# Second half's inputs among the states of the first scan, first half's routing among those of the second, and GpSimd's products of two batches exchanged

## The reference

```python
xz = rmsnorm(x) @ in_proj_w ; xi, z = split(xz)       # 256 channels each
xi = silu(causal_conv4(xi) + conv_b)
dbc = xi @ x_proj_w                                   # 64 dt, 16 B, 16 C
delta = softplus(dt @ dt_proj_w + dt_proj_b)
h[n] = exp(delta * A[n]) * h[n] + delta * xi * B[n]   # 16 states n, over 512 tokens
y = sum_n C[n] * h[n] + D_skip * xi
r = x + (y * silu(z)) @ out_proj_w
out = r + sum of 2 of 8 experts of rmsnorm(r), by the router's weights
```

## Time and profile before

| | us |
|---|---|
| median of 3 runs | 719.82 |
| lowest, highest | 719.0, 720.14 |
| the profiled execution | 721.8 |
| its span in the profile | 720.0 |
| busy in the span: PE, DVE, ACT, POOL | 568.5, 486.4, 385.1, 330.1 |
| TensorE's mean granted clock | 0.92 of full speed |

### The profile page before, as it was taken

The page is one execution under the profiler, slowest core; times in us unless marked ns, Lnnn a source line. Parts: engine busy times, 40 slices in busy tenths (PEclk is TensorE's granted clock), DMA queues, the critical chain, the costliest instruction groups (busy, mean ns, idle before and its releaser), DMA issues.

```text
span 720.0 us, 11031 instructions
## 1 busy us (share of the span) xinstructions
PE 568.5 (79%) x3428; PEld 360.5 (50%) x3447; DVE 486.4 (68%) x1310; ACT 385.1 (53%) x604; POOL 330.1 (46%) x289
## 2 busy tenths in 40 slices
PE   1948587789356776878999899956789989988787
PEld 1413233344112222477989799933555544545366
DVE  5639999944799799643633565387777787886053
ACT  1586555615755455255675566623355665556741
POOL 5249989900599999322578432433012012112010
PEclk9977998799699899889999999985999999999999
DMA  5836565400387765130114200422103103000001
GB/s 141 282 103 196 161 175 164 143 0 7 121 269 232 211 184 180 31 93 15 38 54 126 85 16 22 120 81 80 35 1 93 21 2 101 8 3 2 2 15 45
DMA packets 50523, 65.91 MB, mean 92 GB/s; under 512 B 7730, under 2 KB 29250, under 8 KB 50210
## 3 DMA queue, kind: packets, MB, share of 16 engines
q1 hardware_dynamic: 45122, 59.27, 28.0%
q0 software_dynamic: 2496, 5.15, 1.9%
q10 hardware_dynamic: 2848, 0.78, 0.5%
HBM read 47.46 MB, written 9.52 MB: 79 GB/s over the span
## 4 chain that ended last, share of the span: by engine, by line
PE 33%; POOL 11%; DVE 10%; issue 9%; ACT 4%; ACTq 1%; DMA 0%; POOLq 0%; another core or an unknown queue 0%; DVEq 0%
PE ps L1509 30%; POOL arena L823 4%; DVE arena L1429 3%; POOL moe_out L808 2%; POOL moe_rows L800 2%; ACT arena L1058 2%; POOL arena L835 2%; PE ps L1769 1%; DVE x L1364 1%; DVE nb L1157 1%; DVE arena L1290 1%; DVE stats L1144 1%; POOL arena L849 1%; ACT r L1058 1%; PE ps L1776 1%
## 5 line engine op out<-in xcount | busy, mean ns | idle before, releaser
L1509 PE MATMUL ps<-arena 128*128 128x128 f32 (+10 forms) x2131 | 317.7, 326 | 45.8 <-DVE arena L1429 18.2
L1509 PEld LDWEIGHTS ps<-arena 128*128 128x128 f32 (+2 forms) x2150 | 207.2, 158 | 126.7 <-issue 55.4
L1509 PE MATMUL ps<-arena,ident 128*128 128x512 f32 x256 | 141.6, 703 | 67.0 <-DVE arena L1300 67.0
L1290 DVE TENSOR_TENSOR_SCAN arena<-ps,arena 128x512 f32<-128x512 f32 x128 | 147.9, 1202 | 10.2 <-POOL arena L823 7.2
L1429 DVE CUSTOM_DVE_ANT_0 arena<-ps,cmask 128x128 f32<-128x128 f32 (+3 forms) x256 | 111.3, 487 | 26.4 <-PE ps L1509 25.4
L1509 PEld LDWEIGHTS ps<-arena,ident 128*128 128x128 f32 x256 | 53.9, 222 | 150.2 <-DVE arena L1300 95.3
L999 ACT ACTIVATE ps<-arena 128x512 f32<-128x512 f32 x128 | 87.9, 689 | 73.6 <-DVE arena L1290 73.5
L823 POOL TENSOR_TENSOR arena<-arena 128x1024 f32<-128x1024 f32 x64 | 126.9, 2003 | 0.6
L1058 ACT ACTIVATE arena<-ps 128x1024 f32<-128x1024 f32 (+3 forms) x86 | 57.0, 709 | 37.9 <-PE ps L1509 37.5
L808 POOL DMA_INDIRECT moe_out<-arena,xT x46 | 44.9, 976 | 69.6 <-DVE arena L1453 56.3
L787 POOL TENSOR_TENSOR small<-small,neghalf 128x4 f32<-128x4 f32 (+1 forms) x18 | 22.2, 1236 | 116.3 <-DVE small L1380 75.1
(11 more groups left out here) (191 smaller groups left out, 610.1 us busy)
## 6 DMA issues: line engine op xcount, KB each, us to landing
arena<-bc_rows SPq DMA_DIRECT2D x128, 256.0 KB, 3.9
arena<-arena SPq DMA_DIRECT2D x64, 64.0 KB
arena<-arena SPq DMA_DIRECT2D x28, 128.0 KB, 2.4
moe_rows<-arena SPq DMA_DIRECT2D x2, 1495.0 KB, 11.7
arena<-moe_rows SPq DMA_DIRECT2D x8, 325.0 KB, 5.0
arena<-in_L_attn_a_Wg SPq DMA_DIRECT2D x8, 256.0 KB, 4.9
arena<-in_L_attn_a_Wu SPq DMA_DIRECT2D x8, 256.0 KB, 5.1
arena<-moe_out SPq DMA_DIRECT2D x4, 512.0 KB, 4.3
```

Source lines behind the costliest of these rows:

```text
L1290: V.tensor_tensor_scan(hst[:, g % STATES, e, :], bank(6 + e), dBx[:, g % RING, e, :], 0.0, ALU.mult, ALU.add).then_inc(s_scan, 1)
L1509: return T.matmul(o, l, rr, start=start, stop=stop)
```

## The change

- **Inputs ahead.** The in_proj matmuls and the diagonal-matmul convolution of half 1 are made among the states of half 0, through PSUM bank 5, at the states in AHEAD; ScalarE copies each result at the states in COPY_AT, z into a new buffer `zr` (over weights' staging space that is free by then). Silu of all of them comes after the states (`inputs_1`). VectorE's convolution (`conv_1`) of half 1 comes after the last product of half 0, ahead of the gate.
- **Close of half 0 later.** out_proj of half 0 stands behind x_proj and dt_proj of half 1 on TensorE; VectorE's residual and moments stand between the two deltas.
- **Routing among the states.** h2_norm, transposes, router, softmax, top 2, ranks and slots of half 0 are made in batch 2, at the states in ROUTE_AT. The scatters, from state 2 of batch 2 on before, are at the 16 states of batch 3. Small operands of the routing move to PSUM.
- **Products.** GpSimd makes six in batch 2 and two in batch 3.
- **Rows.** The B and C rows of a half's second batch are stored after the first three states' B rows; each batch waits for its own. One semaphore counts all expert weights.

The diff, cut to its core (new functions that only hold moved lines are left out: `conv_1`, `form_delta`, `add_residual`, `row_copy`, `relu_abs`, `exp_log`, `x_proj`, `dt_proj`, `taps`, `inputs_0`):

```diff
+        z_at = at[0] - 11 * P - 2 * 3 * HID
+        zr = arena[:, z_at:z_at + CT * HL].rearrange("p (e l) -> p e l", e=CT)
...
-        ridf = carve([2, TH])
-        req = carve([2, TH, NE])
+        ridf = ps[:, 4, 64:64 + 2 * TH].rearrange("p (k t) -> p k t", k=2)
+        req = (ps[:, 4, 128:128 + TH * NE].rearrange("p (t e) -> p t e", t=TH), carve([TH, NE]))
...
-        ON_POOL, POOL_LAG, SUM_LAG = ((1, 3, 6, 8, 11, 13), (1, 3, 6, 8, 11, 13), (5, 10), (1, 3, 6, 8, 11, 13)), 2, 2
+        ON_POOL, POOL_LAG, SUM_LAG = ((1, 3, 6, 8, 11, 13), (1, 3, 6, 8, 11, 13), (1, 3, 6, 8, 11, 13), (5, 10)), 2, 2
...
+        AHEAD = {1: ("xi", 0, 0), 3: ("xi", 0, 1), 5: ("xi", 1, 0), 7: ("xi", 1, 1), 9: ("taps", 0, 0), 10: ("taps", 0, 1),
+                 13: ("z", 0, 0), 15: ("z", 0, 1), 17: ("taps", 1, 0), 18: ("taps", 1, 1), 21: ("z", 1, 0), 23: ("z", 1, 1)}
+        COPY_AT = {3: ("xi", 0, 0), 5: ("xi", 0, 1), 7: ("xi", 1, 0), 9: ("xi", 1, 1), 12: ("taps", 0, 1),
+                   15: ("z", 0, 0), 17: ("z", 0, 1), 20: ("taps", 1, 1), 23: ("z", 1, 0), 25: ("z", 1, 1)}
+        first_1 = NS * HB
+        ROUTE_AT = {"h2norm": first_1 + 3, "h2turn": first_1 + 4, "input": first_1 + 6, "router": first_1 + 7,
+                    "logits": first_1 + 9, "top_a": first_1 + 10, "exp": first_1 + 11, "top_b": first_1 + 12,
+                    "rank": first_1 + 13, "slots": first_1 + 15}
...
+            def store_rows(b):
+                sp.wait_ge(s_dts, b + 1)
+                sp.dma_start(bc_rows[b], dts[RK:RK + 2 * NS, b % HB, :]).then_inc(s_bt, 16)
+
             for h in range(HB):
-                for b in range(HB * h, HB * h + HB):
-                    sp.wait_ge(s_dts, b + 1)
-                    sp.dma_start(bc_rows[b], dts[RK:RK + 2 * NS, b % HB, :]).then_inc(s_bt, 16)
                 first, end = state_of(HB * h, 0), state_of(HB * h + HB, 0)
-                sp.wait_ge(s_bt, 16 * HB * (h + 1))
                 for g in range(first, end):
+                    if g == first:
+                        store_rows(HB * h)
+                        sp.wait_ge(s_bt, 16 * (HB * h + 1))
+                    elif g == first + BS:
+                        store_rows(HB * h + 1)
+                    elif g == first + NS:
+                        sp.wait_ge(s_bt, 16 * (HB * h + 2))
...
+                        if h and c == 0 and n == 2:
+                            powers(0, 2 * TB)
+                        j = c * NS + n - NS
                         if h and 0 <= j < 2 * TH:
                             scatter(0, j // 2, j % 2)
-                powers(2 * TB * h, 2 * TB)
+            powers(2 * TB, 2 * TB)
...
+            def inputs_1():
+                act.wait_ge(s_cvc, HB)
+                act.wait_ge(s_zc, 2 * HB)
+                for c in range(HB):
+                    cs = slice(c * L, c * L + L)
+                    S.activation(xc[:, 0, cs], xc[:, 0, cs], ACT.Silu, bias=convb[:, 0:1]).then_inc(s_xc, 1)
+                for e in range(CT):
+                    for c in range(HB):
+                        cs = slice(c * L, c * L + L)
+                        S.activation(zr[:, e, cs], zr[:, e, cs], ACT.Silu).then_inc(s_zs, 1)
+                for c in range(HB):
+                    act.wait_ge(s_cd, HB + c + 1)
+                    S.activation(xc[:, 1, c * L:c * L + L], v[:, c, 1, :], ACT.Silu, bias=convb[:, 1:2]).then_inc(s_xc, 1)
+                row_copy(1, 0)
+                S.preload_act_table_set("natural_log_exp_and_others")
+                relu_abs(1, 0)
+                row_copy(1, 1)
+                exp_log(0)
+                relu_abs(1, 1)
+                exp_log(1)
+
+            def copy_ahead(what, c, e):
+
+                cs = slice(c * L, c * L + L)
+                if what == "xi":
+                    act.wait_ge(s_ip, 8 + 2 * c + e + 1)
+                    S.copy(xip[:, c, e, 4:4 + L], bank(5)).then_inc(s_xi, 1)
+                elif what == "z":
+                    act.wait_ge(s_ip, 12 + 2 * c + e + 1)
+                    S.copy(zr[:, e, cs], bank(5)).then_inc(s_zc, 1)
+                else:
+                    act.wait_ge(s_cv, HB + c + 1)
+                    act.wait_ge(s_dx, c + 1)
+                    S.copy(xc[:, 0, cs], bank(5)).then_inc(s_cvc, 1)
+
+            for h in range(HB):
+                (inputs_0, inputs_1)[h]()
...
+                        if g in COPY_AT:
+                            copy_ahead(*COPY_AT[g])
+                        if g == ROUTE_AT["input"]:
+                            moe_input(0)
+                            moe_input(1)
+                        if g == ROUTE_AT["logits"]:
+                            logits(0)
+                        if g == ROUTE_AT["exp"]:
+                            router_exp(0)
...
+                if h == 0:
+                    for b in range(HB):
+                        conv_1(b)
+                    for b in range(HB):
+                        form_delta(b)
+                else:
+                    form_delta(HB)
+                    add_residual(0)
+                    form_delta(HB + 1)
...
+                        if g == ROUTE_AT["h2norm"]:
+                            h2_norm(0, count["var"])
+                        if g == ROUTE_AT["top_a"]:
+                            top_a(0)
+                        if g == ROUTE_AT["top_b"]:
+                            top_b(0)
+                        if g == ROUTE_AT["slots"]:
+                            find_slots(0, rank_bank(0))
                 weigh(state_of(HB * h + HB, -1))
+                if h == 0:
+                    conv_1(HB)
+                    conv_1(HB + 1)
...
+            def out_proj(h):
+                pe.wait_ge(s_yg, 2 * h + 2)
+                for c in range(HB):
+                    for j in range(TB):
+                        for e in range(CT):
+                            last = mm(ps[:, (0, 6)[h] + c, j * P:j * P + P], zs[:, e, c * L + j * P:c * L + j * P + P],
+                                      opw[:, e, :], start=(e == 0), stop=(e == CT - 1))
+                    last.then_inc(s_op, 1)
+
...
+            def inputs_1():
+                pe.wait_ge(s_wpc, NPREP)
+                pe.wait_ge(s_xc, 2 * HB + 3)
+                x_proj(1, 0)
+                dt_proj(1, 0)
+                pe.wait_ge(s_xc, 2 * HB + 4)
+                pe.wait_ge(s_zc, 2 * HB)
+                x_proj(1, 1)
+                dt_proj(1, 1)
+                out_proj(0)
+
+            def ahead(what, c, e):
+
+                if what == "xi":
+                    pe.wait_ge(s_dl, HB)
+                    wait(pe, s_xi, 2 * HB + 2 * c + e if c or e else 0)
+                    mm(bank(5), ipw[:, e * P:e * P + P], mamba_in(1, c)).then_inc(s_ip, 1)
+                elif what == "z":
+                    if e:
+                        pe.wait_ge(s_zc, 2 * c + 1)
+                    else:
+                        pe.wait_ge(s_cvc, c + 1)
+                    mm(bank(5), ipw[:, (2 + e) * P:(3 + e) * P], mamba_in(1, c)).then_inc(s_ip, 1)
+                elif e == 0:
+                    pe.wait_ge(s_xi, 4 * HB)
+                    wait(pe, s_zc, 2 * c)
+                    taps(bank(5), c, (0, 1))
+                else:
+                    taps(bank(5), c, (2, 3)).then_inc(s_cv, 1)
+
...
-                if h:
-                    rank(h - 1)
-                wait(pe, s_sl, h)
+                wait(pe, s_r, HB * h)
...
+                    if g in AHEAD:
+                        ahead(*AHEAD[g])
+                    if g == ROUTE_AT["h2turn"]:
+                        pe.wait_ge(s_dl, NB)
+                        turn_h2(0)
+                        turn_h2(1)
+                    if g == ROUTE_AT["router"]:
+                        router(0)
+                    if g == ROUTE_AT["rank"]:
+                        rank(0)
...
+            out_proj(1)
```

More of the change, by code:

```diff
@@ L980, in _ @@
                 S.preload_act_table_set("natural_log_exp_and_others")
-                if h:
-                    router_exp(h - 1)
                 for c in range(HB):
-                    b = HB * h + c
-                    for e in range(CT):
-                        act.wait_ge(s_dtp, 2 * b + e + 1)
-                        last = S.activation(u[:, c, e, :], bank(DT[c] + e), ACT.Abs, bias=dtb[:, e:e + 1])
-                        S.activation(bank(DT[c] + e), bank(DT[c] + e), ACT.Relu, bias=dtb[:, e:e + 1])
-                    ch.link(last)
-                    ch.link(S.activation(u[:, c, :, :], u[:, c, :, :], ACT.Exp, scale=-1.0))
-                    S.activation(u[:, c, :, :], u[:, c, :, :], ACT.Ln, bias=1.0).then_inc(s_u, 1)
+                    relu_abs(0, c)
@@ new lines, in add_residual, with h2_norm @@
+                dve.wait_ge(s_r, HB * h + HB)
+                sl = tiles_of(h)
+                moments(r, HB * h, 2 * TB)
+                ch.link(V.tensor_tensor(small[:, 3, sl], mv[:, sl, 0], mv[:, sl, 0], ALU.mult))
```

(26 more changed lines are left out.)

186 lines of the change are left out of this document (77 added, 109 removed).

## The result

The changed kernel takes **715.38 us** (median of 4 runs, 714.11 to 716.03), the kernel before 719.65 beside it (4 runs, 719.0 to 720.14): ratio 0.9933 [0.9917, 0.9949]. Faster, as forecast, but by 4.3 us where 13.3 were forecast, and above the range of 701 to 713. The profiled execution took 715.82 us, its span is 713.9.

A forecast was written before the change was run, and what follows sets the result against it. VectorE bounds the states, GpSimd too in batches 0 and 2; a TensorE, ScalarE and VectorE chain bounds the gap. -22.2 + 2.0 - 0.4 + 8.3 - 1.0 = -13.3 us, from 719.82 to 706.5; range 701 to 713.

The forecast's parts named there:

- Part 3: Batch 2: 8.4 us of routing enter VectorE's stream, more products go to GpSimd, scatters leave; 56.1 against 56.5, -0.4 us.
- Part 1: Gap between the halves: in_proj and TensorE's taps leave it, so 44.5 becomes 22.3 us, -22.2 us.
- The gap: Last product of half 0 to first scan of half 1: -22.2 us, ended by out_proj and VectorE's residual.
- the clock as a rival: Gap: TensorE runs it at the lower clock, +7 us, 713.5 us in all; chance 0.12.
- The first scan: Batches 0 and 1: moved matmuls and ten ScalarE copies cost +2.0 us, bounds 0 and 6.
- The all-copies-exposed rival: Batches 0 and 1: all ScalarE copies of the moved inputs cost time, +4 us, 710.5 us in all; chance 0.12.
- Batch 2: States of batch 2: batch 0's pace of 47.7 plus 8.4 us of routing, 56.1 against 56.5, -0.4 us.
- Batch 3: States of batch 3: four more products on VectorE, all scatters on GpSimd, stalls on dBx; 57.8 against 49.5, +8.3 us.
- the upper bound: Longest time allowed for batch 3: 62 us, with batch 2's whole idle time.
- The close: End of the scan: TensorE's lag shrinks, with no GpSimd products after state 10; -1.0 us, bounds 0 and -1.9.

The follow-up runs named there:

- the kernel with all of it away: Changed kernel with GpSimd's power after batch 2's first dBx, h2_norm on ScalarE, and the softmax's maxima and sums in PSUM: 704.67 us, ratio 0.9785.
- first experiment: Changed kernel with GpSimd waiting for h2_norm's end before its product of state 35: 710.02 us, ratio 0.9859.
- after: The changed kernel itself, against the kernel before: 715.38 us, ratio 0.9933.
- the three added products: Kernel before the change with three GpSimd products, results unused, added behind the power of h2_norm in the gap: 723.62 us, ratio 1.0045.
- products as before: Changed kernel with GpSimd making two products in batch 2 and six in batch 3 again: 723.59 us, ratio 1.0045.

## Why the prediction was wrong, point by point

**The step that failed** is the pricing of VectorE's moved instructions: in Part 3 "h2_norm 1.66, top_a 0.5 [...] 8.4 us, all on the engine that bounds", and in Part 1 "the second addition starts at +17.3, variance at +21.0". Both prices were read where GpSimd stood still (the earlier trace rows has it busy 6.08 of 44.5 us) and carried to places where, by the prediction's own count, it is at work: it has dBx ready at +19.6, between that addition and the variance, and works 50.3 of batch 2's 56.1 us. Measured there: 6.21 for 1.66, and from the second addition's start to the end of the statistics 6.13 us for 3.65. With these 8.5 us found, the sum of the prediction is nearly made whole: the kernel with all of it away took 704.67 against the 706.5 forecast. That it lies 1.8 us below comes from h2_norm's own 1.66 us, which are off VectorE there, and from differences of a microsecond or two in stages that no edit touches: so near an agreement is in part luck.

The Trainium skill states this rule ("SBUF — State Buffer", section "Who interferes with whom"): VectorE in a 2-port mode, which `tensor_scalar` can enter, and GpSimd share one pair of ports, which whoever issues first has for the whole instruction; and VectorE with two SBUF inputs contends with a GpSimd instruction that reads SBUF. The exclusion is what the runs show, that ports cause it is the page's word. They agree: 8 scalings 1.66 us in the kernel before and 6.59 with GpSimd's three products beside them, a two-input instruction 1.39 against 0.22 once one operand is in PSUM, the reduction just ahead of it 0.18 and 0.20 there, ScalarE undisturbed. The page was not weighed in the prediction, and it was the rule that spoke against these two places.

**The gap**: -18.4 for -22.2. The blocked statistics cost 2.5 us and the clock 1.6; the rest was 0.4 us shorter than forecast (21.9 for 22.3 with both away). The prediction had the clock as a rival at 0.12 with +7 us. That rival held in a small part only: one stretch of 5.6 us had a mean of 0.70, the whole gap 0.93. That the chain ends by out_proj, residual and delta, with GpSimd ready before it, was right: GpSimd's first dBx was there at about 168.9, the scan started at 174.12.

**The first scan**: +1.6 for +2.0, right in place and nearly in size. Single states are 0.2 to 0.6 us longer, at 7, 9, 12, 20, 23 and 25 as named (not at 5), and at 17, which was not; those at 13 and 14 are shorter by 1.0 together. So 2.6 us were lost where the prediction counted 3.4, and 1.0 hidden where it took 1.4. The all-copies-exposed rival is out.

**Batch 2**: +3.4 for -0.4. The structure held: once h2_norm is hardly blocked (first experiment), batch 2 takes 56.5 us against 56.1 forecast. But the blocked time in after is 6.1 us (4.55, 1.17 and 0.35) for a miss of 3.8: the forecast for the rest was about 2 us too long, and that hid a part of the miss. One part of it can be named: batch 0, whose 47.7 us it took, has 1.4 us of idle VectorE, and batch 2 of after 0.5.

**Batch 3**: +8.9 for +8.3, and the stalls fell where the walk through the states put them: at 56, at 60 and at 61. VectorE first, then the dBx of GpSimd that it got:

```profile
262.58 1.22 DVE L1387 TENSOR_TENSOR_SCAN arena<-ps,arena 128x512 f32<-128x512 f32 x1 [1.17 <-ACT ps L1054]
...
275.44 1.22 DVE L1387 TENSOR_TENSOR_SCAN arena<-ps,arena 128x512 f32<-128x512 f32 x1 [0.44 <-ACT ps L1054]
...
280.94 1.22 DVE L1387 TENSOR_TENSOR_SCAN arena<-ps,arena 128x512 f32<-128x512 f32 x1 [2.04 <-issue]
```

```profile
260.49 2.01 POOL L843 TENSOR_TENSOR arena<-arena 128x1024 f32<-128x1024 f32 x1
...
278.84 2.02 POOL L843 TENSOR_TENSOR arena<-arena 128x1024 f32<-128x1024 f32 x1
```

1.17, 0.44 and 2.04 us for 1.2, 0.4 and 2.1. The profile names ScalarE, or nothing, as the releaser. But ScalarE's last decay before 262.58 ended at 262.14. The dBx ended at 262.50 in the one case and at 280.86 in the other, 0.08 us before the scan: the ends tell what the label doesn't. One reading behind the bounds was wrong: the "8.4 idle us of batch 2" include 2.64 us that lie before 191.90, in the gap. The earlier trace rows leaves 5.8 (56.50 less 50.72), which would have put the upper bound at about 59.6 and not 62; the forecast itself doesn't use it.

**The close** gave 1.5 us for 1.0: VectorE waits 2.1 us for TensorE's sum there in place of 3.6. **Not foreseen**: -1.0 us before the first state and +0.9 in the rest; neither has a cause that was looked for. Between the ten profiles the first scan starts anywhere from 48.6 to 50.3 us, and the last part scatters by over 3 us, so both may be nothing. The median's offset from the profiled execution (2.0 us before, 0.4 after) makes the remaining 1.6 us between 706.5 and 715.38.

## What to carry to other kernels

A duration on VectorE belongs to a place as well as to an instruction: before moving it next to GpSimd's work, ask whether it has an operand in PSUM. If not, price the first at what is left of GpSimd's instruction and each one after it at a whole GpSimd instruction, as long as GpSimd has one ready; or give one operand to PSUM, move the work to ScalarE, or make GpSimd wait a moment. And compare the mean duration of the same instruction in two traces, since this loss stands in no list of waits: the engine looks busy.

## What the runs showed of the hardware

- A row of small VectorE instructions is blocked more than once: eight scalings, 1.66 us together when GpSimd is idle, took 6.21 to 6.59 us. One of them was made per GpSimd instruction: the longest of after lasted 2.39 us (0.97 and 2.03 us its neighbours), those beside the three added products 1.90 to 1.93, and all others 0.27 to 0.28. How it goes with longer VectorE instructions was not tried.
- Not every instruction is blocked: beside dBx the moments took 1.65 and 0.64 us, as they do without GpSimd, and the reduction L1270 0.18, while L1271 right behind it took 1.39. All of these but L1271 read one tensor.
- GpSimd's own instructions hardly change for it (2.00 and 2.35 us). Where a scaling was under way first, a dBx took 2.09 us in place of 2.00 (products as before, at 186.89). So the price falls on the engine with the short instructions.
- A matmul's price at the lower clock: the same eight took 3.87 us at 1.00 and 5.52 at 0.70.
- ScalarE's first activation after a table load starts at once, here too, in the gap of after:

```profile
154.88 1.28 ACT L1024 ACT_TABLE_LOAD   x1
156.18 0.69 ACT L978 ACTIVATE arena<-ps,arena 128x512 f32<-128x512 f32 x1
```

The 1.38 us that the Trainium skill adds for each switch ("ScalarE: Activation LUTs", "What ACT_TABLE_LOAD costs") don't show at this place either: the copy ahead of the load ended at 154.87.
